# Three of twelve one-hots made by GpSimd instead of VectorE, in a four-layer attention and point-cloud kernel

## What is computed

```python
x = attn0(x, ctx)     # chunked attention (8 heads, chunks of 64) + residual + layer norm
x = attn1(x, ctx)     # full attention, 32 query heads, 8 key heads, low-rank parts on every weight, residual
x = attn2(x, ctx)     # as attn0 with other weights
x = L3(ctx, x)        # point cloud: a batch of 32, 1024 points
```

```python
pd  = 2 * einsum('bdn,bdm->bnm', p, p) - xx[:, :, None] - xx[:, None, :]
idx = top_k(pd, 30)[1]                      # 30 nearest of 1024
rel = pts[bidx, idx] - pts[:, :, None, :]   # 3 coordinates of each neighbour, relative
# rel -> spherical features -> three small layers with batch norm -> softmax -> weighted sum of x
```

## Time and profile before

| what | value |
|---|---|
| median of three executions | 7549.87 us (7542.38 to 7550.98) |
| span of the profiled execution | 7535.0 us |
| median less span | 14.9 us |
| instructions | 210218 |

### The profile page before, as it was taken

The page is one execution under the profiler, slowest core; times in us unless marked ns, Lnnn a source line. Parts: engine busy times, 40 slices in busy tenths (PEclk is TensorE's granted clock), DMA queues, the critical chain, the costliest instruction groups (busy, mean ns, idle before and its releaser), DMA issues.

```text
span 7535.0 us, 210218 instructions
## 1 busy us (share of the span) xinstructions
PE 6930.1 (92%) x79430; PEld 4871.2 (65%) x79430; DVE 6030.7 (80%) x8892; ACT 4370.1 (58%) x10453; POOL 2663.1 (35%) x3399
## 2 busy tenths in 40 slices
PE   8999999999999999999999999999999495888888
PEld 4666666666666666666666666666666232888888
DVE  5888888888888888888888878888887468777776
ACT  3666565556565655665555556565565035666666
POOL 2444444444444444444444444444444200111110
PEclk9999999999898999999889989999898698999999
DMA  3222222111122222221222212121122402222222
GB/s 111 71 64 66 66 66 66 63 64 63 63 70 74 69 67 69 70 67 63 67 67 63 67 63 66 63 69 64 63 64 66 117 0 61 71 64 61 62 62 54
DMA packets 301195, 498.89 MB, mean 66 GB/s; under 512 B 103794, under 2 KB 217602, under 8 KB 299490
## 3 DMA queue, kind: packets, MB, share of 16 engines
q1 hardware_dynamic: 246541, 389.18, 17.2%
q10 hardware_dynamic: 53589, 95.21, 4.1%
HBM read 410.03 MB, written 74.30 MB: 64 GB/s over the span
## 4 chain that ended last, share of the span: by engine, by line
PE 78%; DVE 7%; issue 6%; ACT 4%; POOL 3%; DMA 1%; DVEq 0%; ACTq 0%; POOLq 0%; SPq 0%
PE MISC L708 7%; PE PD L683 6%; PE PD L807 6%; PE SCA L906 6%; PE PD L1156 5%; PE TP L877 4%; PE SCA L1143 3%; PE TP L871 3%; PE SCB L849 3%; PE SCB L838 3%; PE SCA L838 3%; PE SCB L1143 3%; PE TP L761 3%; PE SCA L849 2%; DVE gat L2030 2%
## 5 line engine op out<-in xcount | busy, mean ns | idle before, releaser
L1695 DVE MAX8 m<-pd 128x8 f32<-128x1024 f32 x1024 | 1247.1, 1218 | 133.0 <-issue 72.9
L1701 DVE FIND_INDEX8 idx<-m,pd 128x8 uint32<-128x1024 f32 x1024 | 1248.0, 1219 | 0.4
L525 POOL TENSOR_TENSOR prod<-prod,hm 128x480 f32<-128x480 f32 x384 | 416.7, 1085 | 2261.9 <-ACT prod L1330 2251.1
L1705 DVE MATCH_REPLACE8 pd<-m,pd 128x1024 f32<-128x1024 f32 x768 | 928.0, 1208 | 0.0
L708 PEld LDWEIGHTS MISC<-ptab,gat 128*128 128x128 bf16 x23400 | 644.4, 98 | 161.1 <-issue 98.9
L2030 DVE TENSOR_TENSOR gat<-maskT,con 120x2048 f32<-120x2048 f32 x256 | 584.2, 2322 | 201.6 <-PE SCA L1143 198.0
L1211 ACT ACTIVATE pd<-PD,xxcol 128x512 f32<-128x512 f32 x514 | 361.9, 704 | 634.8 <-PE PD L684 634.8
L708 PE MATMUL MISC<-ptab,gat 128*128 128x24 bf16 x23400 | 659.3, 175 | 47.0 <-DVE gat L1645 47.0
L683 PE MATMUL PD<-arena 128*128 128x512 f32 x1028 | 632.6, 700 | 56.5 <-ACT pd L1211 48.7
L1310 ACT ACTIVATE S<-SCA,mx 128x64 f32<-128x64 f32 (+1 forms) x2560 | 587.7, 358 | 154.0 <-DVE mx L1717 153.6
L1310 ACT ACTIVATE S<-SCB,mx 128x64 f32<-128x64 f32 (+1 forms) x2560 | 597.2, 419 | 35.6 <-DVE mx L1717 35.6
(11 more groups left out here) (271 smaller groups left out, 15573.1 us busy)
## 6 DMA issues: line engine op xcount, KB each, us to landing
gat<-low_scratch SPq DMA_DIRECT2D x396, 640.0 KB, 3.9
arena<-in_ctx ACTq DMA_DIRECT2D x33, 512.0 KB, 3.4
x_scratch<-arena ACTq DMA_DIRECT2D x33, 512.0 KB, 3.3
x3T_scratch<-reg ACTq DMA_DIRECT2D x33, 512.0 KB, 3.4
maskT<-in_mask SPq DMA_DIRECT2D x32, 512.0 KB
arena<-in_x ACTq DMA_DIRECT2D x32, 512.0 KB, 4.8
reg<-in_ctx ACTq DMA_DIRECT2D x32, 512.0 KB, 3.5
arena<-x3T_scratch SPq DMA_DIRECT2D x32, 512.0 KB, 5.9
```

The source lines that it names most:

```text
L1695: V.max(m, buf[:, :]).then_inc(search_step, 1)
L1701: last = V.max_index(idx[:, t, 8 * r:8 * r + 8], m, buf[:, :])
L1705: V.match_replace(buf[:, :], m, buf[:, :], -3.0e38).then_inc(search_step, 1)
```

## The change

GpSimd makes the one-hots of the groups 3, 6 and 9, with a semaphore of its own: that of group 3 between `consume(0)` and `consume(1)`, that of group 6 between `consume(3)` and `consume(4)`, that of group 9 between `consume(6)` and `consume(7)`. VectorE's three calls go. The loads stay where they are. `fill` waits for the semaphore of the engine that made its group. The twelve one-hots behind the loop stay with VectorE.

```diff
+POOL_OH = (3, 6, 9)
...
+        oh_pool = sem("oh_pool")
...
+                def onehot(n):
+
+                    pool.wait_ge(oh_ld[n % NOH], i * (16 * GROUPS // NOH) + 16 * (n // NOH) + 16)
+                    settle(pool)
+                    G_.tensor_scalar(oh[n % NOH], oh[n % NOH], iota_p, None, ALU.is_equal).then_inc(oh_pool, 1)
+
                 pool.wait_ge(split_ready, i + 1)
                 sides(i, 0)
                 consume(i, 0)
+                onehot(3)
                 consume(i, 1)
                 sides(i, 1)
                 sides(i, 2)
...
                 consume(i, 2)
                 consume(i, 3)
+                onehot(6)
                 consume(i, 4)
                 consume(i, 5)
                 consume(i, 6)
+                onehot(9)
                 consume(i, 7)
...
             def fill(i, n, place, ahead=0):
 
-                pe.wait_ge(oh_done, i * GROUPS + n + 1)
+                own = GROUPS - len(POOL_OH)
+                if ahead:
+                    pe.wait_ge(oh_done, i * own + n + 1)
+                elif n in POOL_OH:
+                    pe.wait_ge(oh_pool, i * len(POOL_OH) + POOL_OH.index(n) + 1)
+                else:
+                    pe.wait_ge(oh_done, i * own + n + 1 - sum(p < n for p in POOL_OH))
                 pe.wait_ge(nb_used, i * GROUPS + n + 1 - ahead)
...
                 normalise(2)
                 search(2)
-                onehot(i, 3)
                 search(1)
                 normalise(3)
...
                 scaled(0, X1)
-                onehot(i, 6)
                 search(2)
                 front(1, 0)
...
                 front(1, 5)
-                onehot(i, 9)
                 search(2)
                 front(1, 6)
```

## The result

| | before | after |
|---|---|---|
| median (lowest to highest) | 7546.12 us (7532.33 to 7550.98), 4 executions | 7627.36 us (7618.04 to 7641.59), 4 executions |
| profiled execution: span | 7535.0 us | 7619.4 us (device time 7621.85) |
| TensorE busy | 6930.1 us | 7002.3 us |
| span less TensorE busy | 604.9 us | 617.1 us |
| mean granted clock of TensorE | 0.918 | 0.908 |

The changed kernel is slower: ratio 1.0111, 95% interval 1.0081 to 1.0142. The new lines stand 2 to 17 further down: VectorE's one-hot is 1662, the GpSimd one 584, `consume` 527 to 531, `fill` 725, `normalise` 1746, `scaled` 1786, the turn of its result 906.

What follows compares the result with a forecast made beforehand. TensorE, busy 92% of the span, was taken as the bound. 23 us of waits in twelve short rounds on a 7535.0 us span gave 7558; 14.9 us from span to median made 7573 us, range 7505 to 7740.

Steps and rivals of the forecast that it cites:

- The bound: Whole kernel: TensorE, busy 92% of the span, sets the end; VectorE counts only where TensorE or ScalarE waits for it.
- the relief at nothing: VectorE's list: removing 96 one-hots, 84 us, gains nothing, since VectorE's own later waits for TensorE hide it.
- The price: One one-hot of 2560 columns on GpSimd: 6.9 us, from line 459's 2.6 ns a column; bounds 2.3 and 16.2 us.
- Long rounds, groups 6 and 9, at nothing: Group 3 in long rounds (gap 9.59 us), group 6 after consume(3), group 9 before consume(7): each costs nothing.
- The 0.8 us that GpSimd was to wait: Group 6, after consume(3): VectorE's scaled starts first, so GpSimd's one-hot is held up 0.8 us, at cost 0.
- The short rounds, step by step: Group 3, gap 4.84 us: consume(1) 2.1 us late, onehot(2) held up, fill(2) waits 1.5 us, normalise's result 0.4 more.
- Sum: 1.9 us in each of 12 rounds, 23 us: Group 3's TensorE waits in the 12 short rounds, the prediction's whole cost: 23 us; this case had chance 0.30.
- Rival 3: Behind the first selection: new waits lower TensorE's clock, short rounds become long, 7.3 us each, 88 in all; 7660 us, chance 0.08.
- rivals 2 and 5: GpSimd one-hot's price: 2, 16.2 us, time 7800 to 8030, chance 0.12; 5, under 5.5 us or no hold-up, 7550, chance 0.13.
- rival 1: Group 6 after consume(3): GpSimd starts before VectorE's scaled, 4 us in 32 rounds, 128 us; time 7700 us, chance 0.23.
- The 14.9 us between span and median: Whole kernel: the runs' median lies 14.9 us above the span, added to 7558 to give 7573 us.

Runs made afterwards that it cites:

- e4: Changed kernel with one-hots 3, 6 and 9 made by nobody, so its output is not the reference's; ratio 0.9986 to the kernel before, 7532.35 us.
- e5: e2 with only 1280 of group 3's 2560 columns compared, so its output is not the reference's; ratio 1.0028 to the kernel before, 7565.11 us.
- e1: Changed kernel with group 3's one-hot back on VectorE, 6 and 9 still on GpSimd; ratio 1.0035 to the kernel before, 7570.63 us.
- e3: Changed kernel with VectorE's onehot(2) moved ahead of normalise(0); ratio 1.0061 to the kernel before, 7589.16 us.
- e9: e3 plus a GpSimd wait for VectorE's scaled ahead of one-hot 6; ratio 1.0116 to the kernel before, 7626.80 us.
- e2: Changed kernel with only group 3's one-hot on GpSimd, 6 and 9 back on VectorE; ratio 1.0171 to the kernel before, 7677.07 us.
- e8: e1 plus a GpSimd wait for VectorE's scaled ahead of one-hot 6; ratio 0.9983 to the kernel before, 7529.87 us.

## Why the prediction was right and wrong

- **The bound, and the relief at nothing: right.** e4 shows it: VectorE 81 us less busy, time the same.
- **The price: right.** 6.75 us for 6.9, and the slope that was read from line 459, 2.6 ns a column, measured 2.53 in e5. So neither the comparison nor the bf16 output makes line 574 dearer; that its stride does was not tested by itself. The rule weighed in the prediction, from the Trainium skill's "GPSIMD Engine Reference", section "4.1 Engine selection", is not borne out for this instruction: VectorE takes 0.88 us for it, GpSimd 6.75.
- **Long rounds, groups 6 and 9, at nothing: right in the places.** In rounds with the gap of 9.6 us `consume(1)` stayed where it was; `scaled` took 0.81 us in all 32 rounds. The reason given, that the load lands at that very time, holds: GpSimd sat idle for that load 14.9 us in 32 rounds. It was given for the long rounds; in the short ones it held only because `fill(3)` was late, and e1 and e3 show the other side there. The place that was missed is VectorE's `onehot(2)` in the long rounds, 2.58 us in place of 0.88, for which `fill(2)` did not wait. The 0.8 us that GpSimd was to wait were 0.3 at most (7044 ns against 6747).
- **The short rounds, step by step: right in the steps.** Gap 6.79 instead of 4.84, so `consume(1)` starts 1.95 us late (2.1 forecast) and ends 2.5 late; `onehot(2)` 3.8 to 4.1 us (4 forecast); `fill(2)` waits 1.15 and the transposes 0.69, 1.84 together, where the sum had 1.9; twelve rounds of this kind (12 forecast).
- **"Sum: 1.9 us in each of 12 rounds, 23 us": this is the term that failed, by more than three times.** The twelve rounds with the short gap took 2083.6 us before and 2149.8 after, 66.2 more, 5.5 each in place of 1.9; and the other nineteen, which were to cost nothing, took 3458.9 and 3476.8, 18.0 more. 66.2 and 18.0 are the 84 us. The prediction took a wait to cost its own length, as if the matmuls behind it took the same time; they did not. 72.2 of the 84.4 us are busy time of the same matmuls.
- **Rival 3 had the mechanism and a chance of 0.08, and half the place.** It looked for the clock in the 20 us behind selection 0, and had all twelve short rounds turn into long ones. In the short round from 1961.3 us the clock of that stretch came to 0.83 from 0.95, not to the 0.52 of long rounds, by the fall at 18 us; other falls lie far behind it. The steps were of 3.5 us, not only of 7.3, and the twelve short gaps stayed.
- **The rest:** rivals 2 and 5 fall with the price; rival 1 is real, and sat in two neighbours of the change instead of in the change. The 14.9 us between span and median were no start and end of the program: in after, device time less span of one execution is 2.5 us, so the rest was the difference between executions.
- **Luck in the range.** The direction was forecast, with 0.64. The range held by its upper half, which stood there for rival 1 at 7700 and the clock at 7660; the sum's 7573 and its own range, 7550 to 7595, did not hold, and where the sum had 23 us the median rose by 81. That 7627 lies inside is luck as far as the sum goes.

**What stays open.** Why one version's rounds fall into the longer kinds and another's do not. e9 has nearly the waits of before and the time of after, and a fall of the clock with no wait ahead of it; e2 has fewer moved one-hots and is slower; e5 turns short rounds back and lengthens long ones. That the loss is clock is shown, by the busy time of 79430 matmuls in each ledger row, by the stretches, and by span times clock, the same before and after. That group 3 on GpSimd at its full length sets off most of it is shown by e1, e8 and e5, each without it or with half of it. That `consume(1)`'s lateness alone does so is shown in e9 only together with the 1 us on `fill(3)`. How a microsecond at one place becomes a lower clock 100 us further on was not found, and no forecast of it from the waits would have been sound.

## What to carry to other kernels

Ask first whether the engine to be relieved is late for anybody; leaving its work out, as e4 does, answers that in one run. Moving work to an idle engine then costs its duration there against the gap in each kind of round, the other engine's instructions that it locks out, and the ties that it makes, which a semaphore can settle. Where the matmul engine is busy over 90% and its granted clock varies, split a loss into that engine's idle and busy time before explaining it by waits; in this kernel the waits alone gave a third of the loss in the rounds they hit.

## What the runs showed of the hardware that was not expected

- VectorE's one-hot and `scaled`, both `TENSOR_SCALAR`, are held up when they start inside a GpSimd one-hot until that ends: 0.81 us became 7.28, 0.88 became 4.09; in the first case GpSimd was 0.02 us ahead. The search's `FIND_INDEX8` was not held up there (1.22 us). The Trainium skill has the rule, in "SBUF — State Buffer", section "Who interferes with whom": where a VectorE instruction runs in a two-port mode, whichever of the two engines issues first keeps the shared ports for its whole instruction, and the other is blocked. The trace agrees for these two, and shows that two hundredths of a microsecond decide it.
- Eight matmuls of the same line, 128x128, took 1.09 us in one round and 1.97 in another, with a granted clock of 1.00 and 0.56 in the stretches around them.
- The 31 rounds of every version lie near four lengths, some 3.5 us apart, and few lie between. e9 has rounds at 173.5, 177 and 180.6 us with the same list of instructions.
- A part of the change costs more than the whole: 1.0171 (1.0136 to 1.0206) for group 3 alone, 1.0111 (1.0081 to 1.0142) for all three. Whether the parts add up is less clear: with the tie settled they make 1.0154.
